# Cross-attention with group norm on one core: batch 2's low sum as eight TensorE products instead of four GpSimd adds

## What is computed

```python
q = (Wq @ y + bq).reshape(B, H, Dh, -1)
k = (Wk @ y + bk).reshape(B, H, Dh, -1)
v = (Wv @ x + bv).reshape(B, H, Dh, Lx)
scores = einsum('bhdl,bhel->bhde', q, k) / sqrt(E)
attn = softmax(scores, axis=-1)
out = einsum('bhde,bhel->bhdl', attn, v).reshape(B, E, Lx)
o = Wo @ out + bo + x
mu, var = mean(o, axis=(1, 2)), var(o, axis=(1, 2))
return (o - mu) * rsqrt(var + 1e-5) * gn_w + gn_b
```

## Time and profile before

| | |
|---|---|
| median of 3 runs | 166.63 us (166.38 to 167.06) |
| the profiled execution | 166.47 us |
| its span | 164.6 us |
| PE busy | 154.2 us (94%) |
| DVE busy | 149.5 us (91%) |
| ACT busy | 137.2 us (83%) |
| POOL busy | 98.0 us (60%) |
| GpSimd folds of 128x256 (L252, L263, L274) | 30 each, 729, 729 and 743 ns mean |
| GpSimd last fold (L284) | 30, 474 ns mean |
| DMA | 50.84 MB, mean 309 GB/s |

### The profile page before, as it was taken

The page is one execution under the profiler, slowest core; times in us unless marked ns, Lnnn a source line. Parts: engine busy times, 40 slices in busy tenths (PEclk is TensorE's granted clock), DMA queues, the critical chain, the costliest instruction groups (busy, mean ns, idle before and its releaser), DMA issues. The chain is left out here.

```text
span 164.6 us, 3752 instructions
## 1 busy us (share of the span) xinstructions
PE 154.2 (94%) x932; PEld 121.0 (74%) x932; DVE 149.5 (91%) x686; ACT 137.2 (83%) x354; POOL 98.0 (60%) x162
## 2 busy tenths in 40 slices
PE   7998999999999999999999999999999999998820
PEld 7896887777777788887777777888777777785500
DVE  1788999999999999999999999999999999987861
ACT  3685499999999999999999999999999999767351
POOL 3039267776666676667766666766777666541120
PEclk9999999999999999999999999999999999999995
DMA  5999859999999999998999999999999977631136
GB/s 188 403 407 412 313 196 330 324 338 296 350 342 348 346 357 396 345 336 272 380 377 354 336 344 351 358 334 339 329 374 338 377 308 263 255 127 59 75 127 255
DMA packets 14277, 50.84 MB, mean 309 GB/s; under 512 B 1712, under 2 KB 1712, under 8 KB 14256
## 3 DMA queue, kind: packets, MB, share of 16 engines
q1 hardware_dynamic: 13824, 50.08, 83.3%
q10 hardware_dynamic: 432, 0.53, 0.9%
HBM read 33.82 MB, written 16.78 MB: 307 GB/s over the span
## 5 line engine op out<-in xcount | busy, mean ns | idle before, releaser
L751 PE MATMUL o_ps<-x_sb,m_sb 128*128 128x512 f32 x124 | 61.1, 612 | 0.7 <-ACT out_sb L404 0.7
L751 PE MATMUL g_ps<-hl_sb 128*128 128x258 f32 x256 | 47.0, 308 | 0.0
L484 DVE TENSOR_TENSOR hl_sb<-y_sb,hl_sb 128x512 fp32r<-128x512 f32 x64 | 43.7, 687 | 0.0
L574 DVE BATCH_NORM_STATS2 bn<-o_ps 128x6 f32<-128x512 f32 x62 | 40.3, 685 | 1.4 <-PE o_ps L751 1.4
L325 ACT CAST hl_sb<-y_sb 128x512 fp32r<-128x512 f32 x64 | 39.2, 618 | 1.9 <-DMA y_sb<-in_ctx_dram 1.9
L404 ACT ACTIVATE out_sb<-o_ps,shift,gain 128x1024 f32<-128x1024 f32 x31 | 37.4, 1206 | 2.6
L252 POOL TENSOR_TENSOR lsuma<-hl_sb 128x256 f32<-128x256 f32 x30 | 21.9, 729 | 25.9 <-DVE hl_sb L484 25.9
L751 PEld LDWEIGHTS g_ps<-hl_sb 128*128 128x128 f32 x256 | 35.5, 194 | 0.2 <-DVE hl_sb L484 0.2
L263 POOL TENSOR_TENSOR lsumb<-hl_sb 128x256 f32<-128x256 f32 x30 | 21.9, 729 | 17.5 <-DVE hl_sb L484 17.5
L751 PEld LDWEIGHTS o_ps<-x_sb,m_sb 128*128 128x128 f32 x124 | 21.0, 191 | 14.7 <-issue 14.7
L274 POOL TENSOR_TENSOR lsum<-lsuma,lsumb 128x256 f32<-128x256 f32 x30 | 22.3, 743 | 4.2 <-issue 0.4
(11 more groups left out here) (76 smaller groups left out, 288.9 us busy)
## 6 DMA issues: line engine op xcount, KB each, us to landing
y_sb<-in_ctx_dram SPq DMA_DIRECT2D x32, 512.0 KB, 6.3
x_sb<-in_x_dram SPq DMA_DIRECT2D x32, 512.0 KB, 7.1
out_dram<-out_sb SPq DMA_DIRECT2D x31, 512.0 KB, 6.3
w_in<-in_weights_dram ACTq DMA_DIRECT2D x1, 256.0 KB, 5.4
out_dram<-out_sb ACTq DMA_DIRECT2D x1, 256.0 KB, 2.6
out_dram<-out_sb SPq DMA_DIRECT2D x1, 256.0 KB, 2.8
cols<-in_columns_dram ACTq DMA_DIRECT2D x1, 3.0 KB, 3.4
```

Source lines behind the costliest of these rows:

```text
L484: nc.vector.tensor_tensor(hl_sb[:, b % SLOTS, chunks, C:2 * C], y_sb[:, b % SLOTS, chunks, :], hl_sb[:, b % SLOTS, chunks, 0:C].bitcast(F3 ...
L574: nc.vector.bn_stats(bn[:, b % 2, half, :], o_half(b, half)).then_inc(bn_done, 1)
L751: return nc.tensor.matmul(dst, lhsT, rhs, start=start, stop=stop, **more)
```

## The change

`EARLY` becomes 3, so that batch 2 goes the way of batches 0 and 1. GpSimd's four folds of batch 2 go; its first work is then fold_first(3). TensorE's product of `lsum` with ones for batch 2 goes, and eight products for `low_sum(2)` come between `transpose_cross(2)` and `statistics(-1)`. VectorE gets `copy_high_sum(2)` in the opening, and its `copy_sum(2)` is an add of `early_ps` and `high_sb` instead of a copy. `high_sb` and `early_ps` grow by one batch. Since the helpers compare with `EARLY`, `gram(3, 0)` now waits for `high_copied` in place of `s_copied`, and `low_sum(2)` waits for `s_copied` of batch 1.

```diff
-EARLY = 2
+EARLY = 3
@@ gpsimd, opening
-            fold_second(2)
-            fold_first(2)
-            fold_sum(2)
-            fold_last(2)
             fold_first(3)
             for t in range(4, B + LAGS):
@@ vector, opening
             add_gram(2)
+            copy_high_sum(2)
             invert_sum(1)
@@ tensor, opening
             transpose_cross(2)
+            low_sum(2, range(0, CH))
             statistics(-1)
```

## The result

| | before | changed |
|---|---|---|
| median, 22 runs each | 166.56 us (165.97 to 167.10) | 166.87 us (166.45 to 167.59) |
| ratio to before | | 1.0024 (95%: 1.0014 to 1.0034) |
| the profiled execution | 166.47 us | 166.82 us |
| its span | 164.6 us | 164.5 us |

The change makes the kernel slower by 0.24%. The forecast was 166.47 us, 0.10% faster. The time lies in the stated range, and the move is under the 0.5% that was called no change, but with 22 runs it is clear of the noise, and it goes the wrong way. From a gain of 0.16 us to a loss of 0.31 us some 0.47 us are missing.

What follows compares the result with a forecast made beforehand. TensorE, without idle time in the loop, was taken to carry any shift of its first input product rigidly to the end. That product 0.16 us earlier, other costs zero: 166.63 - 0.16 = 166.47 us, range 166.0 to 167.0 us.

Steps and rivals of the forecast that it cites:

- What bounds the kernel: Steady loop: TensorE has no idle time, so only the first input product's start, 15.42 us, decides the end.
- the pivot column: Opening, VectorE's L566: TensorE waits 0.43 us for it before statistics(-1), the last wait to end.
- the rest_half's 0.69 us: Opening, VectorE: batch 3's second rest_half takes 0.69 instead of 1.22 us without GpSimd's fold_sum(2) over it.
- the folds' new places: Opening, GpSimd: fold_first(3) arrives near 13.05 and ends near 14.15 us; fold_second(3) is issued near 14.12.
- the bad case for L566: Opening, VectorE: L566 waits behind fold_second(3) and is done at 14.86 us, against 14.36 in the good case.
- Parts 2 and 3: Opening: eight TensorE products cost 0.86 us, input product 0.16 us earlier; VectorE's extra copy and add, 0.07 us, cost zero.
- Rival 1: Opening: fold_first(3) gets in before batch 3's second rest_half, L566 ends near 15.15, nothing gained, 166.65 us; 8%.
- Rival 5: Opening, TensorE: eight products quicker than 0.11 us each, so VectorE decides; gain 0.27 us, 166.36 us; 2%.
- the Sum: Whole kernel: 0.16 us off the loop's start, none given back; median 166.63 us becomes 166.47 us, 0.10% faster.
- Parts 3 and 4: VectorE's extra copy and add, and waits that change owner (Gram product, batch 3's sum, load of y): cost zero.
- Rival 2: Loop: one more stall at GpSimd's fold and VectorE's st_in, 0.22 us, giving 166.69 us; 14%; one less 12%.
- Part 2: Opening, TensorE: eight products, 0.86 us, paid by 0.59 us idle and a 0.27 us product; input product at 15.26 us.

Runs made afterwards that it cites:

- a_folds2: Changed kernel with batch 2's four folds put back on GpSimd as dead work, plus 2 GpSimd and 20 VectorE idle memsets: 166.08 us, ratio 0.9986.
- b_p2d2: Kernel before plus 2 idle memsets in GpSimd's opening and 2 in VectorE's, putting its marks where the changed kernel has them: 167.39 us, ratio 1.0035.
- a_both2: Changed kernel plus 6 idle memsets in GpSimd's opening and 20 in VectorE's, a repeat run: 166.04 us, ratio 0.9970.
- b_both2: Kernel before plus 8 idle memsets in GpSimd's opening and 22 in VectorE's, a repeat run: 166.18 us, ratio 0.9973.
- a_p2d2: Changed kernel plus 2 idle memsets in GpSimd's opening and 2 in VectorE's: 165.74 us, ratio 0.9965.
- b_both: Kernel before plus 8 idle memsets in GpSimd's opening and 22 in VectorE's, first run: 166.41 us, ratio 0.9972.

## Why the prediction was wrong

- **What bounds the kernel, and the opening: right.** The wait that ended last was the pivot column. The transpose-to-product distance was forecast as 1.25 us and is 1.23; the rest_half's 0.69 us, the folds' new places and the bad case for L566 came as written. Parts 2 and 3 held, with copy_sum(2) hidden. That GpSimd's folds, not its late sum, held the opening was argued then and is shown by a_folds2.
- **Rival 1** did not happen: the rest_half, issued first, kept its turn. **Rival 5** neither: the eight products took 0.87 us (13.73 to 14.60), 0.11 each. The 81 ns of the Trainium skill's section "Back-to-back issue gap" would have given 0.65; the row of before was right.
- **The step that failed is "none given back" in the Sum.** Parts 3 and 4 put what the change costs outside the opening at zero. The added work does cost nothing there, but its number of instructions does, and the Sum has no term for it. The loop is rigid, as said: its period hangs on nothing but itself. But the pauses in it hang on how many instructions stand ahead of them. Against the kernel before, the changed one has 4.82 for 4.49 us at t = 9, 4.89 us at t = 22 for 4.78 at t = 21, and 0.12 us more in the ending: 0.33 + 0.11 + 0.12 = 0.56, where the whole stretch is 0.55 us longer. Less 0.18 in the opening that makes +0.37 us; the medians have +0.31.
- **Rival 2 was the right one, and was mis-sized: 0.22 us, where 0.55 were given back.** It named the stall, its path through st_in and "both engines' programs get other lengths", and gave 166.69 us with a chance of 14%, as if the stall fell at random. b_p2d2 shows that it doesn't. What was at hand in the trace of before: the pause is at GpSimd's record 196, one of 10 per iteration, the fetch packets are 8 KB; 196 - 128 = 68 is then another mark, in fold_last's slot there, two slots behind fold_sum's. Taking 8 records away puts it into the slot of fold_sum, and moves record 196 out of it: 0.33 us come and 0.26 go (4.78 to 4.52 us), which leaves some 0.1 us of the gain, not a loss. What turned the sign is VectorE, with 0.37 us behind its record 447 and 0.12 in the ending, and of that the trace of before shows only the 0.14 us at record 703.
- **A slip in the ledger that cost nothing.** Part 2 has the eight products' 0.86 us paid for by 0.59 us of idle time and 0.27 us of the product on the fold. By that nothing would be gained. The durations overlap; only the differences of starts count, 1.25 us for 1.41, and the forecast went by these.
- The median of 166.87 us lies in the range of 166.0 to 167.0 us, and "within 0.5%" held.

The Trainium skill, "Runtime: NRT & Kernel Launch", section "Instruction fetch mechanics", says that an engine's instruction memory is refilled in blocks of 16 KiB, 256 instructions, while the current ones run, and that crossing a boundary costs little and is mostly hidden. Here "mostly hidden" holds (each of GpSimd and VectorE passes more marks than cost time), and queue 8 has packets of 16 KB (0.11 MB in 7), but queue 14 has packets of 8 KB, the marks of GpSimd and VectorE lie 128 instructions apart, and the three pauses of the changed kernel that aren't hidden cost 0.8 to 1.0 us together (139.89 against 138.93 to 139.10). The measurement decides.

## What to carry to other kernels

In a program written out without loops, an edit of a few instructions moves every later mark of 128 instructions of that engine, and on an engine that others wait for a badly placed mark cost some 0.3 us here; before an effect of a few tenths of a per cent is put down to the edit's content, pad the shorter program by some idle instructions and see whether it stays. And where GpSimd and VectorE share work on the same data, moving a fold off GpSimd may pay by what it frees on VectorE, even if nobody waits for the fold.

## What the runs showed of the hardware

**Pauses at marks 128 instructions apart.** They lie behind GpSimd's records 68 and 196 and VectorE's 447 and 703; seven kernels show one, and in the loops of all eleven whose traces can be compared none stands at another count, whatever the time (fold_sum behind record 68 starts at 35.86, 36.16, 40.05 or 40.50 us). It is 0.26 us at VectorE's add_query_bias and 0.30 to 0.36 us at fold_sum. At the other marks it was not visible: on fold_last, on a wait for VectorE, behind a 0.69 us operation, and at VectorE's records 63 to 575 in the kernel before. Why fold_last hides it and fold_sum doesn't can be read from the records of waits. Ahead of fold_sum stands a wait of its own (record 195 in the kernel before), which ends at 94.43 us, 0.04 us after fold_second: when the mark is reached, nothing is left for GpSimd to do. The wait ahead of fold_last is over at once (0.02 us at 35.81), so that the mark is reached while fold_sum runs for 0.73 us and covers the pause. VectorE's marks at add_query_bias and at L626 also lie right behind such a wait. This fits all the traces, but no run was made for it. Nor do the runs part the fetch from anything else that goes by the same count, the recording of the profile included: each execution on record was recorded with its span.

**TensorE's start.** The first products run at about half the rate until some point in the first microseconds, and that point differs from run to run. In the kernel before, the products of the first Gram matrix start 0.21 to 0.22 us apart up to 6.76 us and 0.12 us apart from 6.92 us on, and the trace's record of the full clock begins at 6.85 us; in the changed kernel it begins at 4.65 us, in the other traces compared at 4.99 to 7.22. (The windows print a PEclk of 1.00 for the time before the record as well.) The same eight products took

```profile
5.60 1.35 PE L748 MATMUL g_ps<-hl_sb 128*128 128x258 f32 x8
```

in the changed kernel and 1.89 us at 5.55 in the kernel before; a_both2 has 1.36 us, and b_both2, its twin without the change, 1.99. They end 0.49 us earlier in the changed kernel, which is enough for the 0.42 us by which its transpose stood earlier. In the other traces the transpose starts at 13.45 to 14.04 us with the change and at 13.89 to 14.16 without. Since the changed kernel's median is no better for it, I take it for chance of the profiled execution; that it makes a good part of the spread of single runs is a guess, and it wasn't tried by itself.

**The version to keep** is a_p2d2, 165.74 us, 0.35% under the kernel before (0.21 to 0.48%), of which the traces put 0.18 us on the change's opening and 0.40 us (139.33 to 138.93) on marks that no longer cost anything. Most of it can be had without the change: b_both and b_both2, the kernel before with idle memsets, stand at 0.9972 and 0.9973.
